# A GNN layer followed by a mixture-of-experts layer on one core: four expert items per turn right behind the last gather, no index translation there, and epochs of 62, 22 and 14 node tiles instead of 54, 30 and 14

## The chip, the cores and the metric

The kernel runs on one core of one Trainium2 chip. The metric is the time of the whole program on the device in microseconds (us). TensorE is called PE here and its weight loads PEld; VectorE is DVE, ScalarE is ACT, GpSimd is POOL, and SyncE is SP, which in this kernel only issues DMAs. SPq, ACTq and POOLq are the instruction streams that issue DMAs.

## What is computed

There are 12,500 nodes with 256 features each and 212,500 weighted edges, sorted by their target node. Everything is float32.

```python
x = x + gnn(layernorm(x), src, dst, edge_weight, W, b)
#   msgs = f[src] * edge_weight; agg = segment_sum(msgs, dst); agg @ W.T + b
x = x + ffn(layernorm(x), gate_w, gate_b, W1, b1, W2, b2)
#   probs = softmax(x @ gate_w + gate_b); the two largest of 8 experts are kept
#   out  += prob[e] * (gelu(x @ W1[e] + b1[e]) @ W2[e] + b2[e])   (256 -> 512 -> 256)
```

## The kernel before, in words

**Tiles and turns.** The edges are cut into 208 groups of 1,024 (`NG`), the nodes into 98 tiles of 128 (`NT`). A planner (`plan`) writes out a list of turns before the kernel is built. Every engine's program is the same list of turns, each engine doing its own part in a fixed order, and semaphores tie them together. A turn below 208 is "busy": POOL gathers the 1,024 source rows of one group with eight indirect DMAs (`gather`, L523), DVE makes the eight 128x80 masks of the group (L1366), PE multiplies them with the rows (`sums`, L885), and the 80 sums are turned and added into a ring of node columns (L875, L1379). `rows` has three buffers, so POOL can be up to three groups ahead of PE.

**Nodes.** When all edges of a tile are in, the tile goes through the linear layer (`linear`, L905), the second layernorm (`node` on DVE, `normalise` on ACT) and the gate (`turn_node` L924, `logits` L933). Tiles are routed in parts (`SIZES`, 2 to 8 tiles): `softmax`, `choose`, `rank` (PE, L941), `place` (DVE) decide for each token which expert's queue it goes to and at which row.

**Queues.** Each tile is then sorted by expert on PE (`sort`, L913), copied by ACT (L1123) and stored to a staging area in memory; from there `copy_some_runs` (L504) copies eight runs, one per expert, into the queues `slots`. SP issues them; from tile 92 on SP and POOL issue four each. `send` is SP's name for it.

**Items.** A block of 128 queued tokens of one expert is an item. An item is open when all its tokens are sure to be sent. It takes four steps: SP loads it and its expert's first matrix (`load_xi`, L688 and L691), PE turns it (`turn_xi`, L949), `up` multiplies it with W1 (L962), `gelu` on ACT (L1166), `down` multiplies with W2 (L978), and `result` on DVE adds the bias and scales (L1590, L1593). In the planner a step is a tuple `(a, b, c, entering)`: item `a` goes down, `b` up, `c` is turned and `entering` is loaded. In a busy turn there is one step, or two in every second turn while more than six items wait; in a turn behind the last gather there are two, and three once all tiles are sent. There are 217 items.

**Epochs and results.** The tiles are cut into three epochs (`EPOCH_SIZES`). Queues are filled up to whole blocks at the end of an epoch, so that the results of one epoch can be read back while later ones are still built. Results of the first two epochs go to memory by item (`store_y`, `yq`). A node's two results are found by `index_results` on DVE (L1604 to L1608, called the translation here) and fetched by POOL with two indirect DMAs per tile (`gather_results`, L564): one tile per busy turn (`got`), four tiles per turn, called a batch, behind the last gather (`pairs`, made of the same `rows` and `got` buffers). DVE adds them to the node's row (L1612, L1614) and SP stores the output (L747, L720). Results of the third epoch are scattered instead, one indirect DMA per item (`scatter_result`, L551), and read at the very end (`finish_late`, L738): SP issues those reads when all scatters and the output stores of the last three batches have landed.

The order inside a turn behind the last gather is written in `tail_turn`, once for each engine. There SP loads all the turn's items first and sends tiles after that. A tile that is routed and sent within the same turn stands in `t.quick`; `t.index` are the tiles translated in the turn.

## Time and profile before

| | before |
|---|---|
| median of 3 runs | 2578.02 us (2567.03, 2578.02, 2579.33) |
| the profiled execution | 2568.56 us, span 2566.9 us |
| mean granted TensorE clock | 0.91 |
| busy: PE, POOL, PEld, DVE, ACT | 81%, 70%, 63%, 62%, 25% of the span |
| last gather of source rows issued | 2290.20 us |
| last scatter of a result issued | 2541.52 us |

The span runs from the first to the last instruction; the execution's own time is 1.7 us longer. The busy share is that of instructions at work: an indirect DMA counts 0.95 us on POOL, but the next one starts 1.25 us after it, so a POOL that does nothing but issue them shows 76%.

### The profile page before, as it was taken

The page shows a single profiled execution, that of the slowest core. Times are in us where ns is not written, and L with a number is a line of the kernel's source. Part 1 is how long each engine was busy: PE and PEld are TensorE (multiplying, and loading weights), DVE is VectorE, ACT ScalarE, POOL GpSimd, SP SyncE. Part 2 cuts the span into 40 slices and gives each one's busy share as a digit, 9 for nine tenths or more (in the row PEclk, how much of TensorE's full clock was granted, in tenths as well). Part 3 has the DMA queues.
Part 4 walks back from the last instruction along what each step waited for, and adds up shares of the span by engine and source line. Part 5 has one row for each costly group of instructions (what it writes and reads, how often), then busy time and mean ns, then how long its engine had stood idle before and what let it go on. Part 6 is the DMA issues. An engine that isn't in the chain of part 4 may idle for free.

```text
span 2566.9 us, 46927 instructions
## 1 busy us (share of the span) xinstructions
PE 2069.9 (81%) x11178; PEld 1625.8 (63%) x11179; DVE 1591.4 (62%) x6566; ACT 653.7 (25%) x1900; POOL 1802.5 (70%) x1909
## 2 busy tenths in 40 slices
PE   4666786688899889888897899896978878886595
PEld 2444564477677677765775678674757666765485
DVE  7888546446565465465666756776776656776344
ACT  3332111122222122221321223221223222232131
POOL 7665777777777777777767767577777777752473
PEclk8776888899999999998999999998989889998797
DMA  8766755867868879778788699597889788795696
GB/s 285 250 206 211 233 176 167 258 217 250 292 215 272 262 222 293 255 233 271 221 263 274 200 302 299 171 307 251 272 275 315 230 272 281 262 284 199 221 370 227
DMA packets 304350, 646.04 MB, mean 252 GB/s; under 512 B 62536, under 2 KB 197226, under 8 KB 291402
## 3 DMA queue, kind: packets, MB, share of 16 engines
q1 hardware_dynamic: 145320, 325.55, 37.4%
q0 software_dynamic: 90384, 248.17, 32.2%
q10 hardware_dynamic: 68370, 69.23, 7.7%
q8 instruction: 100, 1.64, 0.3%
q14 instruction: 176, 1.44, 0.2%
HBM read 543.70 MB, written 208.20 MB: 293 GB/s over the span
## 4 chain that ended last, share of the span: by engine, by line
POOL 26%; PE 19%; DVE 18%; issue 14%; DMA 11%; SPq 11%; ACT 1%; DVEq 1%; ACTq 0%; POOLq 0%
POOL rows L523 22%; SPq L504 8%; PE bank L885 7%; DMA slots<-stage 5%; PE bank L978 5%; PE bank L962 4%; DMA stage<-sorted_x 3%; POOL got L564 2%; DVE spread L1366 2%; DVE bn L1345 2%; SPq L454 1%; PE bank L905 1%; DVE pre_bn L1322 1%; DVE square_n L1413 1%; POOL rows L564 1%
## 5 line engine op out<-in xcount | busy, mean ns | idle before, releaser
L523 POOL DMA_INDIRECT rows<-xhat,src_t x1488 | 1423.0, 956 | 500.8 <-issue 446.2
L885 PE MATMUL bank<-rows,spread 128*80 128x256 f32 x3328 | 870.4, 421 | 163.4 <-DMA rows<-xhat,src_t 70.8
L885 PEld LDWEIGHTS bank<-rows,spread 128*80 128x80 f32 x3328 | 548.7, 168 | 445.7 <-issue 200.7
L978 PE MATMUL bank<-w,hT 128*128 x1736 | 439.1, 398 | 46.3 <-DVE y_sb L1593 29.0
L962 PEld LDWEIGHTS bank<-xiT,w 128*128 128x128 f32 x3472 | 423.9, 193 | 28.6 <-issue 8.2
L962 PE MATMUL bank<-xiT,w 128*128 128x128 f32 x3472 | 427.7, 277 | 9.8 <-ACT xiT L1150 5.6
L1166 ACT ACTIVATE hT<-bank,b1T 128x128 f32<-128x128 f32 x868 | 247.6, 368 | 672.7 <-PE bank L962 455.5
L978 PEld LDWEIGHTS bank<-w,hT 128*128 128x128 f32 x1736 | 326.8, 198 | 101.0 <-issue 61.7
L1379 DVE TENSOR_TENSOR acc<-acc,bank 128x160 f32 x208 | 66.9, 322 | 506.8 <-PE bank L875 455.7
L1366 DVE TENSOR_SCALAR spread<-iota_w,dst_rel,wgt 128x80 f32<-128x80 f32 x1488 | 366.2, 338 | 0.2
L523 POOL DMA_INDIRECT rows<-in_x,src_t x176 | 168.4, 957 | 75.9 <-issue 51.0
L1590 DVE TENSOR_TENSOR y_sb<-bank,b2B 128x256 f32<-128x256 f32 x217 | 91.5, 422 | 181.2 <-PE bank L978 171.6
L1110 ACT ACTIVATE sums_n<-bank 80x256 f32<-80x256 f32 x186 | 69.7, 375 | 385.8 <-PE bank L885 385.6
L913 PE MATMUL bank<-xs,sort_mask 128*128 128x272 f32 x392 | 133.5, 423 | 29.7 <-DVE sort_mask L1532 25.6
L1116 ACT ACTIVATE xs<-x_t,shift,rstd 128x256 f32<-128x256 f32 x98 | 59.3, 605 | 344.2 <-DVE shift L1416 340.0
L564 POOL DMA_INDIRECT got<-yq,gather_i x120 | 115.7, 964 | 36.6 <-issue 36.3
L875 PE MATMUL bank<-ident,sums_n 80*128 80x80 f32 x416 | 68.6, 247 | 82.1 <-ACT sums_n L1108 51.0
L905 PE MATMUL bank<-gnn_wT,acc 128*128 128x256 f32 x392 | 109.5, 404 | 19.9 <-DVE acc L1379 19.9
L1123 ACT ACTIVATE sorted_x<-bank 128x272 f32<-128x272 f32 x196 | 77.4, 395 | 169.9 <-PE bank L913 158.1
L875 PEld LDWEIGHTS bank<-ident,sums_n 80*128 80x128 f32 x416 | 49.3, 144 | 106.8 <-ACT sums_n L1108 53.9
L949 PE MATMUL bank<-ident,xi 128*128 128x128 f32 x434 | 85.3, 279 | 36.5 <-DMA xi<-slots 36.5
L933 PEld LDWEIGHTS bank<-gate_wS,xnT 128*128 128x128 f32 x392 | 59.5, 208 | 83.6 <-ACT xnT L1140 80.8
(191 smaller groups left out, 1893.3 us busy)
## 6 DMA issues: line engine op xcount, KB each, us to landing
w<-in_w SPq DMA_DIRECT2D x217, 512.0 KB
slots<-stage SPq DMA_DIRECT2D x760, 136.0 KB
xi<-slots SPq DMA_DIRECT2D x217, 136.0 KB
stage<-sorted_x ACTq DMA_DIRECT2D x98, 272.0 KB
rows<-xhat,src_t POOLq DMA_INDIRECT x1488
yq<-y_sb ACTq DMA_DIRECT2D x182, 128.0 KB
x_t<-in_x SPq DMA_DIRECT2D x97, 128.0 KB
x_d<-x_t ACTq DMA_DIRECT2D x97, 128.0 KB
```

Of the source, the lines that this page charges most:

```text
L504: eng.dma_start(slots[bass.ds(b, P), :], stages[t % STAGES][bass.ds(a, P), :]).then_inc(done, 16)
L523: pool.indirect_dma_start(rows[q][:, c, :], None, x if g < RAW else xhat, bass.IndirectOffsetOnAxis(ap=src_t[:, g * CG + c:g * CG + c + 1] ...
L564: pool.indirect_dma_start(to[:, c, :], None, yq[0:FIRST_ITEM[EPOCH_OF[PART_OF[t]] + 1] * P], bass.IndirectOffsetOnAxis(ap=gather_i[:, t, c ...
L875: done = nc.tensor.transpose(B_TURN[:, k * W:(k + 1) * W], sums_n[:, k * P:(k + 1) * P], ident[0:W, 0:W])
L885: done = nc.tensor.matmul(B_SUM[0:W, 0:D], spread[g % 2][:, c, :], rows[q][:, c, :], start=c == 0, stop=c == CG - 1)
L905: done = nc.tensor.matmul(B_NODE[:, 0:D], tile(t)[:, k, :], gnn_wT[:, k, :], start=k == 0, stop=k == KD - 1)
L913: nc.tensor.matmul(B_SORT[:, 0:XW], sort_mask[t % 2][:, h * P:(h + 1) * P], xs[:, t % XR, :], start=True, stop=True).then_inc(sort_done, 1)
L962: done = nc.tensor.matmul(bank[:, j * P:(j + 1) * P], w1[:, i % W1B, b, j * P:(j + 1) * P], xiT[i % 2][:, b, :], start=b == 0, stop=b == K ...
L978: done = nc.tensor.matmul(bank[:, 0:D], hT[i % 2][:, j, :], w2[:, bass.ds(e, 1), j, :].rearrange("p o f -> p (o f)"), start=j == 0, stop=j ...
L1166: done = nc.scalar.activation(hT[i % 2][:, j, :], bank[:, j * P:(j + 1) * P], ACT.Gelu, bias=b1T[:, bass.ds(e * KH + j, 1)])
L1366: done = nc.vector.tensor_scalar(spread[g % 2][:, c, :], iota_w[:], dst_rel[:, g * CG + c:g * CG + c + 1], w8[:, c:c + 1] if g < RAW else ...
L1590: nc.vector.tensor_tensor(y_sb[i % YB][:], bank[:, 0:D], b2B[:, bass.ds(e, 1), :].rearrange("p o f -> p (o f)"), op=ALU.add).then_inc(y_bi ...
```

## The change

Three edits and the reordering that they need:

1. `EPOCH_SIZES`: the first epoch has 62 tiles (131 items) in place of 54 (115), the second 22 (51) in place of 30 (67). The third is the same (35 items).
2. In turns behind the last gather, until the last tile is sent, up to four items enter in place of two. The third and fourth step stand behind the sorting of the turn's quick tiles on PE and ACT; on SP their loads stand behind the sending of the quick tiles.
3. The translation is left out of those turns (turns 208 to 210); in the turns behind them two tiles are translated per turn.

```diff
-EPOCH_SIZES = ((6, 8, 8, 8, 8, 8, 8), (8, 8, 6, 4, 4), (4, 4, 2, 2, 2))
+EPOCH_SIZES = ((6, 8, 8, 8, 8, 8, 8, 8), (8, 8, 6), (4, 4, 2, 2, 2))
...
-        n_steps = (1 + (waiting > 6 and tau % 2 == 0)) if busy else 2 if NK - 1 not in sent_at else 3
+        n_steps = (1 + (waiting > 6 and tau % 2 == 0)) if busy else min(4, max(2, waiting)) if NK - 1 not in sent_at and with_sums else 3
...
-        while index_next < LATE and len(t.index) < (1 if busy else BATCH):
+        while index_next < LATE and len(t.index) < (1 if busy or not with_sums else 2 if NK - 1 in sent_at else 0):
...
             def tail_turn(plan, t, last_turns, fast, first_batched):   # SP
-                for step in t.steps:
+                for step in t.steps[:2]:
                     if step[3] >= 0:
                         load_xi(step[3])
...
-                for u in ([t.stage] if t.stage >= 0 else []) + t.quick:
-                    send(u)
+                if t.stage >= 0:
+                    send(t.stage)
+                for step in [] if t.quick else t.steps[2:]:
+                    if step[3] >= 0:
+                        load_xi(step[3])
...
+                for u in t.quick:
+                    send(u)
+                for step in t.steps[2:] if t.quick else []:
+                    if step[3] >= 0:
+                        load_xi(step[3])
...
-                for a, b, c, _ in t.steps[1:]:                         # PE
+                for a, b, c, _ in t.steps[1:2]:
                     if b >= 0:
                         up(b, fast)
                     step_down(a, c, fast)
                 for u in t.quick:
                     sort(u, 0)
                     sort(u, 1)
+                for a, b, c, _ in t.steps[2:]:
+                    if b >= 0:
+                        up(b, fast)
+                    step_down(a, c, fast)
```

ACT is split in the same way as PE. The new list of turns differs from the old one as follows. Up to turn 139 nothing moves but translations. The first tile's results are fetched in turn 177 in place of 160, so that 31 tiles are fetched in busy turns in place of 48, and 53 behind them in place of 36 (14 batches in place of 10). Busy turns with two steps are turns 132 to 138, 152 to 172, 184 to 188 and 196 to 206 (each second one) in place of 134 to 154, 166 to 172, 178 to 186 and 194 to 204. 170 items are through at the end of the busy turns in place of 176. The four turns 208 to 211 have 4, 4, 4 and 3 steps in place of 2, 2, 2 and 3, so that both plans stand at the same item (184) at the end of turn 210. The list has 226 turns in place of 225.

The order of the instructions shows it at three places.

PE at the end of turn 208 and the start of turn 209, before. L913 is the sort of tile 93, L941 and L942 rank the part of tiles 92 and 93, L875 turns the last group's sums, L905 is the linear layer of tile 96:

```order
L978 MATMUL bank<-w,hT 128x256
L913 MATMUL bank<-xs,sort_mask 128x272 x2
L941 MATMUL bank<-both,below 128x16
L942 MATMUL bank<-both,ones 128x16
L875 MATMUL bank<-ident,sums_n 128x80 x2
L962 MATMUL bank<-xiT,w 128x128 x8
L905 MATMUL bank<-gnn_wT,acc 128x256 x2
```

The same place in the changed kernel (its lines stand eight further down: L921 is the sort, L957 turns an item, L949 and L950 rank):

```order
L921 MATMUL bank<-xs,sort_mask 128x272 x2
L970 MATMUL bank<-xiT,w 128x128 x8
L957 MATMUL bank<-ident,xi 128x128 x2
L978 TENSOR_LOAD item_be
...
L970 MATMUL bank<-xiT,w 128x128 x8
L957 MATMUL bank<-ident,xi 128x128 x2
...
L949 MATMUL bank<-both,below 128x16
L950 MATMUL bank<-both,ones 128x16
L883 MATMUL bank<-ident,sums_n 128x80 x2
L970 MATMUL bank<-xiT,w 128x128 x8
L913 MATMUL bank<-gnn_wT,acc 128x256 x2
```

Two whole steps, with an item to be turned in each, now stand between the sort and the next turn's rank and linear layer.

SP in turn 208, before, where the copies of the quick tile (L504) are the turn's last transfers but for one output, and the next turn's items follow:

```order
L504 DMA slots<-stage 16x2176
L747 DMA out_nodes<-res 128x256
L454 TENSOR_LOAD item_be
L688 ISA
L688 DMA xi<-slots 128x272
L691 ISA
L691 DMA w<-in_w 128x1024
```

The same place in the changed kernel:

```order
L504 ISA
L504 DMA slots<-stage 16x2176
L454 TENSOR_LOAD item_be
L688 ISA
L688 DMA xi<-slots 128x272
L691 ISA
L691 DMA w<-in_w 128x1024
```

The store of the output has moved ahead of the copies, four loads of items follow instead of two, and the first two of them belong to turn 208 itself: the fourth step of that turn turns the first of them on PE.

POOL at the end of the program, before (L551 scatters results of the third epoch, L564 fetches results):

```order
L551 DMA results<-y_sb,result_i 27136x256 x3
L564 DMA rows<-yq,gather_i 128x256 x8
L551 DMA results<-y_sb,result_i 27136x256 x3
L564 DMA rows<-yq,gather_i 128x256 x4
L551 DMA results<-y_sb,result_i 27136x256 x11
```

The same place in the changed kernel:

```order
L551 DMA results<-y_sb,result_i 27136x256 x3
L564 DMA rows<-yq,gather_i 128x256 x8
L551 DMA results<-y_sb,result_i 27136x256 x3
L564 DMA rows<-yq,gather_i 128x256 x4
L564 DMA got<-yq,gather_i 128x256 x4
L551 DMA results<-y_sb,result_i 27136x256 x2
L564 DMA got<-yq,gather_i 128x256 x2
```

The last eleven scatters had no fetches between them; now fetches go on until behind the last scatter.

## Rows read from the trace of the kernel before

**Rows 1.** The page's busy time of each engine.

```profile
PE 2069.9 (81%) x11178; PEld 1625.8 (63%) x11179; DVE 1591.4 (62%) x6566; ACT 653.7 (25%) x1900; POOL 1802.5 (70%) x1909
```

**Rows 2.** Busy time of each engine by stage; last PEclk, DMA share, GB/s.

```profile
1455.94:1674.54 218.60, 201.06 (x1185) 166.66 (x1184) 146.86 (x583) 62.09 (x196) 143.98 (x152) 0.98 0.78 253
...
1900.88:2293.69 392.81, 334.88 (x1821) 268.46 (x1822) 259.29 (x1060) 101.35 (x304) 298.65 (x310) 0.92 0.83 271
2293.69:2401.69 108.00, 72.11 (x370) 58.76 (x369) 65.38 (x289) 29.08 (x80) 19.53 (x33) 0.83 0.56 179
2401.69:2516.36 114.67, 93.73 (x612) 85.86 (x613) 46.52 (x146) 33.01 (x116) 85.29 (x88) 0.90 0.99 348
```

**Rows 3.** POOL in order of time: turns 160, 177, last busy fetch, tail.

```profile
1684.55 0.95 POOL L523 DMA_INDIRECT rows<-xhat,src_t  x1 [0.30 <-issue]
...
1900.88 0.95 POOL L523 DMA_INDIRECT rows<-xhat,src_t  x1 [0.30 <-issue]
...
2292.73 0.95 POOL L564 DMA_INDIRECT got<-yq,gather_i  x1 [0.30 <-issue]
...
2401.69 1.01 POOL L564 DMA_INDIRECT rows<-yq,gather_i  x1 [0.30 <-issue]
...
2541.52 0.96 POOL L551 DMA_INDIRECT results<-y_sb,result_i  x1 [0.77 <-DVE y_sb L1593]
```

**Rows 4.** POOL's waits for PE in 1455.94-1590.67, to 1674.54, to 2293.69: total, times, longest.

```profile
POOL rows L523 <- PE bank L885: 16.7, 8, 3.9
...
POOL rows L523 <- PE bank L885: 14.8, 4, 8.4
...
POOL rows L523 <- PE bank L885: 0.3, 1, 0.3
```

**Rows 5.** PE in order of time: sums of three successive groups (turns 153 to 155).

```profile
1605.02 3.62 PE L885 MATMUL bank<-rows,spread 128*80 128x256 f32 x16
...
1616.76 3.65 PE L885 MATMUL bank<-rows,spread 128*80 128x256 f32 x16
...
1625.03 1.24 PE L885 MATMUL bank<-rows,spread 128*80 128x256 f32 x5
```

**Rows 6.** PE in order of time behind the last gather.

```profile
2321.88 2.05 PE L905 MATMUL bank<-gnn_wT,acc 128*128 128x256 f32 x4 [5.41 <-DVE acc L1379]
...
2342.15 0.64 PE L924 MATMUL bank<-ident,xs 128*128 128x128 f32 x2
...
2359.80 0.69 PE L949 MATMUL bank<-ident,xi 128*128 128x128 f32 x2 [9.15 <-DMA xi<-slots]
...
2364.23 0.45 PE L941 MATMUL bank<-both,below 128*128 128x16 f32 x2
...
2385.58 0.87 PE L913 MATMUL bank<-xs,sort_mask 128*128 128x272 f32 x2
```

**Rows 7.** DVE in order of time: first translation of turn 208, its last, `place` of turn 211.

```profile
2314.02 0.28 DVE L1604 SCALAR_TENSOR_TENSOR item_hit<-item_all,block_of,item_row 128x67 f32<-128x67 f32 x1
...
2320.05 0.17 DVE L1608 CAST gather_i<-item_of 128x2 int32<-128x2 f32 x1
...
2375.37 0.15 DVE L1477 COPY count_et<-bank 128x16 f32<-128x16 f32 x1
```

**Rows 8.** SP's DMA issues in order of time: start, length, transfer.

```profile
2307.81 12.15 SPq L504 DMA_DIRECT2D slots<-stage  x8
...
2341.81 12.11 SPq L504 DMA_DIRECT2D slots<-stage  x8
...
2355.26 0.33 SPq L688 DMA_DIRECT2D xi<-slots  x1
...
2544.66 6.09 SPq L738 DMA_DIRECT2D rows<-results  x12
```

**Rows 9.** DMA issues by line: count, KB each, median us from issue to landing.

```profile
out_nodes<-res SPq DMA_DIRECT2D x60, 128.0 KB, 4.0
...
rows<-yq,gather_i POOLq DMA_INDIRECT x48, 5.8
```

More of the change, by code:

```diff
@@ L1194, in tail_turn @@
                     copy_sums(t.sums)
-                for _, b, c, _ in t.steps[1:]:
+                for _, b, c, _ in t.steps[1:2]:
                     if b >= 0:
@@ L1206, in tail_turn @@
                     store_sorted(u)
+                for _, b, c, _ in t.steps[2:]:
+                    if b >= 0:
+                        gelu(b, fast)
+                    if c >= 0:
+                        copy_xiT(c)
             def turns(plan, fast):
```

## The prediction

> **What bounds the kernel now.** The page's busy shares come first, and they mislead: PE leads with 81%, POOL has 70% [rows 1]. The list of POOL's instructions in time says otherwise. In busy turns each indirect DMA starts 0.3 us behind the end of the one before, whose reason is "issue", that is, nothing but its own sequencer. The stage table gives the pace: 310 DMAs in 392.81 us, 1.267 us each [rows 2]. A busy turn with a fetch has ten of them, so the 17 turns 160 to 176 take 216.33 us, 12.73 us each [rows 3]; with eight it cannot be below 10.0. The list of POOL's waits then shows where PE ends a wait of POOL: 16.7 us in turns 140 to 151, 14.8 us in turns 152 to 158, and 0.3 us in the 619 us behind that, where the longer turns leave PE slack [rows 4]. So POOL's issue rate sets the busy stage, PE only in patches before the fetches begin.
>
> Behind the last gather the picture has three stages. For 108 us POOL is busy 19.5 us and PE 72.1 [rows 2]: the last tiles are made, routed, sorted and sent, a chain of short steps with many engines. From 2401.69 to 2516.36 POOL issues without a pause again: 88 DMAs in 114.67 us, 1.303 us each. Then come the last scatters, the last at 2541.52 [rows 3], and SP's reads of the scattered results at 2544.66 [rows 8], 22.2 us before the span's end.
>
> **The busy stage: about 30 us shorter.** 17 tiles are no longer fetched there: 34 DMAs x 1.267 = 43.1 us of POOL's issue. This is the gain if POOL stays the bound. PE corrects it. A turn with two steps takes PE 11.74 us from one group's sums to the next, one with one step 8.27 [rows 5]: the double costs 3.5 us. I work out the four patches.
> - Turns 140 to 151 lose their doubles (the planner runs out of open items, since the longer epoch opens its last block later). POOL's 8 waits there, 16.7 us less the usual 0.3 us for each, 14.3 us, go: -14.3.
> - Turns 152 to 158: the 14.8 us, 13.6 net, fall at the routing of a part of eight tiles. The same routing stands there after the change, so nothing goes; two more doubles (156, 158) with sorts beside them: +7.
> - Turns 160 to 163 are now 10 us turns with two doubles and sorts: +7. Doubles without a sort beside them fit, since 11.74 + 8.27 is two turns of POOL.
> - The routing of the next eight tiles (turns 170 to 173) now also falls in 10 us turns. It cost nothing at 12.7 us; at 10 us it cost 13.6 in the patch above: +13.6.
>
> -43.1 - 14.3 + 7 + 7 + 13.6 = -30. The bounds: if PE never makes POOL wait, -43.1 - 27.9 = -71. If each of the nine doubles of turns 156 to 172 costs 3.5, -43.1 - 14.3 + 31.5 + 13.6 = -12. I take -30, as doubles with a sort did cost that much and those without did not.
>
> **The routing chain behind the last gather: about 20 us longer.** Here both plans reach the same item by turn 210, so six items (21 us of PE at 3.5) come in, and twelve translations go out. What the translations cost is seen in DVE: four of them take from 2314.02 to 2320.22, 1.55 us each, and the linear layer of tile 96 waits 5.41 us for the addition behind them [rows 6, 7]. That wait goes. What comes in its place:
> - Turn 208. Two steps are put between the sort of tile 93 and the rank and linear layer of turn 209, 7 us, and the second of them turns an item whose load SP issues only behind the copies of tile 93. These end at 2319.96; an item is turned 4.5 us after its load is issued (2355.26 to 2359.80, [rows 6, 8]). So PE stands at that item until about 2325.5, and behind it on its queue are rank, the last sums' turn and the linear layer. That goes to about 2331 from 2321.88: +9.
> - Turn 209. The same, and worse: the copies of tiles 94 and 95 keep SP for 12.11 us [rows 8], which is 9 us later now, to about 2363; its two loads follow, the item is there at 2369, one more down step, and turn 210's first gate transpose, the one that everything in the routing of tiles 96 and 97 hangs on, is at about 2372 instead of 2342.15 [rows 6]: +30.
> - Turn 210. Before, PE waited 9.15 us here for the item behind these same copies; that wait is now served already. Two more steps cost 7. Rank at about 2391 instead of 2364.23: +27.
> - Turn 211. Before, DVE took 11.1 us from that rank to `place`, of which four translations are 6.2 [rows 6, 7]. They are gone; the listing stays. From `place` to the sort of tile 96 it is 10.2 us as before. Sort at about 2406 instead of 2385.58: +20.
>
> The last stall is the same as before in kind: the third load of turn 211 stands behind the last copies. Bounds: below, the items hide in PE's 35.9 idle us and only the translation's wait goes, -6; above, the whole slip of turn 209 stays, +30. I take +20.
>
> Were the load quicker, less would be lost. The trace has 4.5 us from its issue to the start of the transpose. The Trainium skill, "DMA: Bandwidth & Descriptors", Anatomy of one DMA, gives 2.0 us plus the bytes at 436 GB/s, 2.3 us for 136 KB, fitted on DMAs that GpSimd issues; by that page of the Trainium skill each of the two stalls would be 2.2 us shorter and the chain +16. The row decides here.
>
> **The stage that POOL bounds at the end: about 41 us longer.** POOL starts batch 1 when tile 97 is copied (2401.69 before). From there to the end of the last scatter (2542.48) it issued 64 fetches and 35 scatters in 140.8 us. Now it has 98 fetches (53 tiles, less the four of batch 0) and 35 scatters: 133 x 1.303 = 173.3 us, +32.5. PE needs 3.5 us for an item and has three per turn of about 14 us, so it follows. The 25 us in which POOL used to wait for the last items are filled with fetches. Then the end: the late reads started 2.2 us behind the last scatter. Now the last thing is a fetch, whose landing, addition and output store come first: 5.8 us from issue to landing, of which 0.95 is issue, 0.9 us on DVE, 0.6 us of SP's issue, 4.0 us to land [rows 9]. That makes 10.4, +8.2. Together +40.7. Bounds: +35 if the pace is 1.25 and the store lands at once, +46 if batches wait for buffers.
>
> **Sum.** -30 + 20 + 41 = +31 us on the profiled execution's own 2568.56 (span 2566.9): 2600. The runs shown lie at two places, 2567.0 and 2578 to 2579, the profiled one at the lower; on the median, 2578.0, the sum is 2609. I forecast the middle, 2604. About 0.5% (13 us) is what a measurement of this kernel can tell from no change.
>
> **The rivals.**
> - *The moved items hide.* PE is idle 35.9 us in the 108 us stage [rows 2], the six items need 21. If they fall into its waits, the chain is -6 in place of +20: -30 - 6 + 41 = +5, 2574 to 2583, no change. For it: the room. Against it: PE runs in order, and the loads stand behind SP's copies. The Trainium skill, "Perfetto Trace Analysis", Optimization Strategy, speaks for this rival: where the most-contended engine changes over time, interleaving those regimes may improve performance.
> - *POOL never waits for PE in the busy stage*, so that this is at its bound of -71. That is one mechanism, three row buffers bridging the routing of turns 155 and 172, and it ends on the other side: -71 + 20 + 35 = -16, 2562 on the median. It decides from a busy saving of about 68 us on. Against it: the waits of 8.4 us in just such a turn [rows 4].
> - *More stalls than I count.* A PE that waits comes back slow: the granted clock is 0.83 in the 108 us stage, against 0.98 in the dense one [rows 2], and the DMA share of 0.99 behind it leaves no room for transfers that bunch. Chain +30, busy -20: +51, 2629.
> - *The fetches cost nothing at the end*, because PE is the bound there. Then +8 in place of +41: -2, no change. The row against it is POOL's unbroken issue from 2401.69 to 2516.36.
>
> **How the numbers follow.** My forecast 0.58, more stalls 0.15, items hide 0.11, fetches free 0.04, POOL never waits 0.08, something else 0.04, half of it slower and half faster. Slower 0.75, same 0.15, faster 0.10. The range of 8 in 10 leaves out the upper end of the stalls and most of the faster case: 2574 to 2630; the forecast's own range is 2590 to 2622.
>
> **What the profile of the changed kernel would show.** Right: the last gather of source rows issued near 2260; turns 140 to 151 at 10.0 us with no wait for PE, turns 173 and 174 with waits of 5 to 8 us; PE waiting for `xi` from `slots` in turns 208 and 209; 135 to 145 us from the last busy fetch to POOL's batch 1, against 109; then POOL issuing unbroken for about 170 us, and the late reads some 10 us behind the last fetch. Wrong: a POOL with pauses in that last stage, or a PE without waits for `xi` in turns 208 and 209.

## The result, and the profile after

| | before | after |
|---|---|---|
| median of the runs | 2578.09 us (6 runs, 2567.03 to 2582.58) | 2595.35 us (6 runs, 2588.18 to 2602.12) |
| profiled execution, own time | 2568.56 us | 2600.76 us |
| span of it | 2566.9 us | 2599.2 us |

The changed kernel is slower: ratio 1.0082, 95% interval 1.0064 to 1.0099, so 16 to 26 us. The forecast was 2604 us with 2574 to 2630, slower with a chance of 0.75.

The page's busy line of the changed kernel hardly differs from [rows 1]; it can't tell where 32 us went:

```profile
PE 2076.3 (80%) x11174; PEld 1626.9 (63%) x11175; DVE 1584.5 (61%) x6506; ACT 652.6 (25%) x1897; POOL 1802.2 (69%) x1909
```

Busy time by stage of the changed kernel, columns as in [rows 2]. The stages are turns 140 to 159, turns 160 to 176, the other turns with gathers, the chain behind them, the stage of the batches, and what follows the start of the late reads:

```profile
1453.95:1673.76 219.81, 181.31 (x958) 140.52 (x957) 141.49 (x570) 49.59 (x148) 152.84 (x160) 0.93 0.72 227
1673.76:1875.03 201.27, 183.01 (x1074) 149.94 (x1074) 131.26 (x516) 56.36 (x179) 130.14 (x136) 0.99 0.79 255
1875.03:2268.41 393.38, 323.38 (x1752) 255.86 (x1750) 280.57 (x1120) 99.69 (x295) 298.99 (x310) 0.92 0.86 279
2268.41:2395.05 126.64, 93.73 (x504) 77.27 (x504) 52.52 (x223) 36.94 (x107) 19.55 (x32) 0.84 0.59 191
2395.05:2576.31 181.26, 124.77 (x796) 113.42 (x796) 95.07 (x328) 42.63 (x150) 129.76 (x133) 0.86 0.88 298
2576.31:2599.20 22.89, 0.00 (x0) 0.00 (x0) 8.86 (x10) 0.00 (x0) 0.00 (x0) 0.50 0.73 236
```

Against [rows 2, 3, 8]: everything up to the end of turn 207 is 25.3 us shorter (2268.41 for 2293.69), the chain 18.6 us longer (126.64 for 108.00), the stage of the batches 38.3 us longer (181.26 for 142.97), and the rest 0.7. The sum is +32.3, the difference of the two spans. In the fifth row GpSimd issues 133 DMAs in 181 us, as counted in the prediction.

GpSimd's waits for TensorE in turns 140 to 151, 152 to 159, 160 to 176 and behind them (total, times, longest), which answer to [rows 4]:

```profile
POOL rows L523 <- PE bank L893: 7.7, 2, 7.4
...
POOL rows L523 <- PE bank L893: 11.8, 3, 6.5
...
POOL rows L523 <- PE bank L893: 33.6, 13, 7.2
...
POOL rows L523 <- PE bank L893: 0.6, 2, 0.3
```

The third row is new: 33.6 us in thirteen waits, where before had one, of 0.3 us. The first row is not empty, as the prediction had it: a wait of 7.4 us stays in turn 141. TensorE behind the last gather, which answers to [rows 6]: the item of turn 208 whose load is late, the linear layer of tile 96, the late item of turn 209, the gate transpose of tile 96, the rank, and the sort of tile 96.

```profile
2297.98 0.69 PE L957 MATMUL bank<-ident,xi 128*128 128x128 f32 x2 [4.58 <-DMA xi<-slots]
...
2305.76 1.10 PE L913 MATMUL bank<-gnn_wT,acc 128*128 128x256 f32 x4 [0.58 <-DVE acc L1396]
...
2342.85 0.69 PE L957 MATMUL bank<-ident,xi 128*128 128x128 f32 x2 [9.14 <-DMA xi<-slots]
...
2347.28 0.40 PE L932 MATMUL bank<-ident,xs 128*128 128x128 f32 x2
...
2365.30 0.29 PE L949 MATMUL bank<-both,below 128*128 128x16 f32 x2
...
2377.55 0.86 PE L921 MATMUL bank<-xs,sort_mask 128*128 128x272 f32 x2 [4.18 <-DVE sort_mask L1549]
```

SyncE's queue shows why the second item is late: its load (2337.59) stands behind the copies of tiles 94 and 95, which answer to the 12.11 us of [rows 8].

```profile
2325.64 11.24 SPq L504 DMA_DIRECT2D slots<-stage  x8
2337.59 0.34 SPq L688 DMA_DIRECT2D xi<-slots  x1
```

The item is turned 5.26 us after that issue (2342.85).

### The profile page after: what moved, and what is told of

Same layout as the page of the kernel before. It is cut to its first block, busy times and chain, and to the rows that moved or that the text cites. A ratio compares the mean times of both kernels' runs of the same rounds, so it can differ in the third digit from the quotient of the medians.

```text
span 2599.2 us, 46816 instructions
## 1 busy us (share of the span) xinstructions
PE 2076.3 (80%) x11174; PEld 1626.9 (63%) x11175; DVE 1584.5 (61%) x6506; ACT 652.6 (25%) x1897; POOL 1802.2 (69%) x1909
## 4 chain that ended last, share of the span: by engine, by line
POOL 23%; PE 19%; DVE 17%; issue 14%; DMA 13%; SPq 11%; ACT 1%; DVEq 1%; ACTq 1%; POOLq 0%
POOL rows L523 19%; SPq L504 9%; PE bank L893 8%; DMA slots<-stage 7%; PE bank L986 4%; PE bank L970 4%; DMA stage<-sorted_x 2%; POOL got L564 2%; DVE spread L1383 2%; DMA rows<-xhat,src_t 1%; DVE bn L1362 1%; POOL rows L564 1%; SPq L454 1%; PE bank L913 1%; POOL results L551 1%
## 5 line engine op out<-in xcount | busy, mean ns | idle before, releaser
L921 PE MATMUL bank<-xs,sort_mask 128*128 128x272 f32 x392 | 133.5, 423 | 27.4 <-DVE sort_mask L1549 23.3
L564 POOL DMA_INDIRECT got<-yq,gather_i x104 | 100.9, 970 | 31.7 <-issue 31.7
L913 PE MATMUL bank<-gnn_wT,acc 128*128 128x256 f32 x392 | 110.1, 405 | 12.9 <-DVE acc L1396 12.9
L957 PE MATMUL bank<-ident,xi 128*128 128x128 f32 x434 | 85.3, 279 | 34.7 <-DMA xi<-slots 34.6
L941 PEld LDWEIGHTS bank<-gate_wS,xnT 128*128 128x128 f32 x392 | 58.9, 206 | 85.5 <-ACT xnT L1152 83.0
```

The lines of the kernel that those rows point to most:

```text
L564: pool.indirect_dma_start(to[:, c, :], None, yq[0:FIRST_ITEM[EPOCH_OF[PART_OF[t]] + 1] * P], bass.IndirectOffsetOnAxis(ap=gather_i[:, t, c ...
L913: done = nc.tensor.matmul(B_NODE[:, 0:D], tile(t)[:, k, :], gnn_wT[:, k, :], start=k == 0, stop=k == KD - 1)
L921: nc.tensor.matmul(B_SORT[:, 0:XW], sort_mask[t % 2][:, h * P:(h + 1) * P], xs[:, t % XR, :], start=True, stop=True).then_inc(sort_done, 1)
```

## The experiments

Every kernel was timed against the kernel before on the same chip; those named e and those named f in the table ran on two different chips, so they are compared by these ratios. To read them I cut each profile at three events: the end of the last gather of source rows on GpSimd; GpSimd's copy behind its last wait of 4 to 7 us for earlier copies to land, 2.8 us ahead of its next fetch; and the start of SyncE's late reads. For the changed kernel the first two are

```profile
2264.73 0.94 POOL L523 DMA_INDIRECT rows<-xhat,src_t  x1 [0.30 <-issue]
...
2392.28 0.49 POOL L504 DMA_DIRECT2D slots<-stage  x1 [6.10 <-DMA slots<-stage]
```

| kernel | ratio to before (95%) | last gather ends | chain | batches | PE matmuls in them |
|---|---|---|---|---|---|
| before | 1 | 2291.2 | 107.8 | 145.8 | 770 |
| changed | 1.0082 (1.0064-1.0099) | 2265.7 | 126.6 | 184.0 | 796 |
| e1, changed with old epochs | 1.0017 (1.0001-1.0033) | 2293.8 | 122.2 | 135.7 | 640 |
| e2, new epochs alone | 1.0032 (1.0016-1.0048) | 2261.9 | 104.8 | 187.2 | 926 |
| e7, translation rule alone | 0.9956 (0.9941-0.9972) | 2294.8 | 89.3 | 150.3 | 770 |
| e3, changed, loads ahead of copies | 1.0005 (0.9989-1.0020) | 2258.1 | 107.5 | 179.7 | 789 |
| f1, changed, half the batch fetches | 1.0001 (0.9987-1.0016) | 2264.0 | 122.0 | 157.6 | 798 |
| f3, e3 with old epochs | 0.9925 (0.9905-0.9945) | 2296.2 | 102.8 | 134.4 | 637 |
| f4, e7 and a batch a turn earlier | 0.9996 (0.9980-1.0011) | 2295.2 | 107.0 | 149.4 | 770 |
| f2, e7 with four epochs | 1.0124 (1.0098-1.0150) | 2352.4 | 91.7 | 142.8 | 770 |

Behind the late reads all have 22 to 23 us. The column of the last gather has its own scatter: kernels whose turns 0 to 207 do the same work lie at 2291.2 to 2296.2 and at 2258.1 to 2265.7. So a difference of 5 us there says nothing.

**e1: the epochs of before put back.**

```diff
-EPOCH_SIZES = ((6, 8, 8, 8, 8, 8, 8, 8), (8, 8, 6), (4, 4, 2, 2, 2))
+EPOCH_SIZES = ((6, 8, 8, 8, 8, 8, 8), (8, 8, 6, 4, 4), (4, 4, 2, 2, 2))
```

> The changed kernel with the epochs of before (54, 30 and 14 tiles): only the third and fourth steps and the translation rule are new. Theory (the chain behind the last gather grew by the extra steps ahead of the sorts, and the epochs alone moved fetches out of the turns with gathers and into the end): the stage with gathers is as before (-2 to +1 us), the stretch from the last gather to the first fetch batch is 17 to 19 us longer, the end is 4 us shorter since more items are through when the batches begin; together 13 to 15 us over the kernel before, a ratio near 1.005. Rival 1 (the extra steps are the whole of the loss and the epochs cost nothing in sum): about +28 to +31 us, ratio 1.011 to 1.012. Rival 2 (extra steps lie in idle time of TensorE): -6 to 0 us.

Measured 1.0017, +4 us (0 to 8). The chain grew by 14.5 us, near what was expected; the stage of the batches fell by 10 us, not 4. The first rival (the steps are the whole loss) is out: with the new epochs in place of the old the same kernel is 17 us slower. Why the items removed were worth so much is taken up under f3.

**e2: the new epochs alone.** The same line changed in the kernel before.

> The kernel before with the epochs of 62, 22 and 14 tiles and nothing else. Theory: the stage with gathers is 25 us shorter, as in the changed kernel (33 fetch instructions fewer ahead of the last gather, less the stalls of new two-step turns), the chain from the last gather to the first batch is as before (within 3 us), and the end takes 42 to 47 us more, since GpSimd issues 33 fetch instructions more there at 1.3 us each; together +18 to +22 us, ratio 1.007 to 1.0085. Rival 1 (GpSimd does not bound the end, and fetches moved there are hidden): -25 us, ratio 0.990. Rival 2 (the epochs are neutral, what GpSimd gains it gives back one for one): 0 us.

Measured 1.0032, +8 us (4 to 12), under the expected 18 to 22. Both parts are there: the last gather 29 us earlier, the batches 41 us longer, the chain 3 us shorter. I had taken 25 and 42 to 47 and hung the expectation on the before's profiled execution, whose last gather is the earliest of the five with old epochs. Averaged over five and four profiles (2294.2 and 2262.4) the epochs bring 31.8 us there.

**e7: the translation rule alone.**

```diff
-        while index_next < LATE and len(t.index) < (1 if busy else BATCH):
+        while index_next < LATE and len(t.index) < (1 if busy or not with_sums else 2 if NK - 1 in sent_at else 0):
```

> The kernel before with the translation rule of the changed kernel alone: none in the three turns behind the last gather, two per turn behind. Theory: VectorE has its translations off the chain there (TensorE's wait of 5.41 us for the sums of tile 96 and VectorE's 6.2 us ahead of the places go), so the stretch from the last gather to the first batch is 6 to 12 us shorter, and nothing else moves: -6 to -12 us, ratio 0.995 to 0.998. Rival: the translations were in idle time of VectorE and the chain is set by the copies to the store and the index loads on the queues: 0 us, ratio 1.000. Second rival: the translations that are late keep GpSimd's batches waiting at the end: +5 us.

Measured 0.9956, -11 us (7 to 15): this part of the change is a gain by itself. TensorE's linear layer of tile 96, the rank and the sort of tile 96:

```profile
2317.48 1.03 PE L905 MATMUL bank<-gnn_wT,acc 128*128 128x256 f32 x4
...
2358.62 0.45 PE L941 MATMUL bank<-both,below 128*128 128x16 f32 x2
...
2371.99 0.62 PE L913 MATMUL bank<-xs,sort_mask 128*128 128x272 f32 x2
```

Counted from the last gather's end these are 22.6, 63.8 and 77.2 us; in before [rows 6] 30.7, 73.1 and 94.4. The wait for the addition is gone, which with what stood around it is 8.1 us, and from rank to sort it is 13.4 us in place of 21.3. That is more than the 6.2 us that the translations take on VectorE. Most of the rest is on TensorE: the eight matmuls of an item's down step, which stand right ahead of that sort, take 3.78 us in before, behind 7.05 us of idle time, and 1.99 us in e7, behind 1.16 us:

```profile
2382.01 3.78 PE L978 MATMUL bank<-w,hT 128*128 x8 [7.05 <-DVE y_sb L1593]
```

```profile
2370.16 1.99 PE L978 MATMUL bank<-w,hT 128*128 x8 [1.16 <-ACT hT L1166]
```

The granted clock is 0.50 in the first of these stretches, the lower of its two levels, and 1.00 in the second. So with the idle time of the wait goes 1.8 us of slower matmuls. Of the chain's 18.5 us, 4.5 are lost again in the batches, where GpSimd waits 24.0 us for item results in place of 18.8.

**e3: the changed kernel, with SyncE issuing all loads of items ahead of its copies.**

```diff
-                for step in t.steps[:2]:
+                for step in t.steps:
                     if step[3] >= 0:
                         load_xi(step[3])
...
-                for step in [] if t.quick else t.steps[2:]:
-                    if step[3] >= 0:
-                        load_xi(step[3])
```

(and the same three lines behind the sends of `t.quick`).

> The changed kernel with SyncE issuing all index loads of a turn ahead of its copies to the store, as the kernel before did, in place of behind them. Theory: the waits of TensorE for the loaded item indices in the two turns behind the last gather (4.58 and 9.14 us) vanish, the copies start 1 to 3 us later; net 7 to 10 us shorter than the changed kernel, ratio to the kernel before near 1.005. Rival 1 (the waits only move: the linear step or the sort that comes next waits for the later copies, or for VectorE): no difference to the changed kernel, ratio 1.008. Rival 2 (the later copies delay the sorted index and then the first batch): +3 us.

Measured 1.0005 against 1.0082: 20 us shorter than the changed kernel, twice what was expected. All of it is in the chain (107.5 for 126.6) and the batches (179.7 for 184.0). The two waits for `xi` are gone, and the same events of TensorE are:

```profile
2291.12 1.10 PE L907 MATMUL bank<-gnn_wT,acc 128*128 128x256 f32 x4 [0.86 <-DVE acc L1390]
...
2338.55 0.29 PE L943 MATMUL bank<-both,below 128*128 128x16 f32 x2
...
2350.82 1.28 PE L915 MATMUL bank<-xs,sort_mask 128*128 128x272 f32 x2 [4.20 <-DVE sort_mask L1543]
```

From the last gather: 33.0, 80.4 and 92.7 us; in the changed kernel 40.1, 99.6 and 111.9. The waits of the rows (4.58 + 9.14) are less than the 19.2 us they cost, because each queue waits for the other: SyncE's copies of tiles 94 and 95 wait for tiles that TensorE sorts, and TensorE stands at an item whose load is behind SyncE's copies. In e3 the third load of turn 209 goes out 35.3 us behind the last gather, in the changed kernel 71.9 (the 2337.59 above); the copies of 94 and 95 start at 52.9 us in e3 and at 60.0 in the changed kernel (2325.64):

```profile
2293.39 0.33 SPq L688 DMA_DIRECT2D xi<-slots  x1
...
2311.04 10.61 SPq L504 DMA_DIRECT2D slots<-stage  x8
```

In e3 the chain is as long as in before, with five to six items more in it (527 matmuls for 385, 26 to an item). TensorE's busy time in it, 91.68 us of 107.45, stands against 72.11 of 108.00 in [rows 2]:

```profile
2258.13:2365.58 107.45, 91.68 (x527) 77.21 (x526) 53.07 (x226) 37.95 (x112) 19.73 (x31) 0.89 0.69 227
```

That does not show the items hidden in TensorE's idle time, since the chain of before also holds the translations. Against e7, which has none either, e3's chain is 18.2 us longer (107.5 for 89.3), close to the 21 us that the prediction gives to six items.

The Trainium skill, "Perfetto Trace Analysis", Optimization Strategy, says that interleaving regimes with different busiest engines may improve performance. By that rule items moved into the chain should pay. Whether they do with the loads in time is read from f3 against e7, below, and by those two the trace agrees, if by little.

**f1: half of the fetches behind the last gather left out.** One of the two results of each of those nodes is left out of the output.

```diff
-                for c in range(2):
+                for c in range(2 if done in got_in else 1):
...
-                dve.wait_ge(batch_got[t.batch % BATCHES], 32 * batch_loads(plan, t.batch))
+                dve.wait_ge(batch_got[t.batch % BATCHES], 16 * batch_loads(plan, t.batch))
```

> The kernel of the run that fetches only one of a node's two results behind the last gather (that result of those nodes is left out of the output), again, on another chip, since the first chip ran every kernel, the one before too, some 36% slower. The expectation stands: with GpSimd's issue as the bound of the last stage, its 53 DMAs fewer take 69 us off until TensorE's own items stop it, 2550 to 2565 us; if TensorE bounds the stage, within 5 us of the changed kernel (ratio 1.008).

Measured 1.0001 against 1.0082, 21 us less, between the theory and its rival. The batches take 157.6 us for 184.0. GpSimd's rows in turn show why they stop there: it waits for item results in every turn.

```profile
2476.90 0.98 POOL L551 DMA_INDIRECT results<-y_sb,result_i  x1 [1.74 <-DVE y_sb L1610]
2478.45 0.97 POOL L551 DMA_INDIRECT results<-y_sb,result_i  x1 [0.56 <-DVE y_sb L1610]
2480.41 0.96 POOL L551 DMA_INDIRECT results<-y_sb,result_i  x1 [0.99 <-DVE y_sb L1610]
```

GpSimd's waits for item results in the stage of the batches (total, times, longest), of before, changed, f1, f3:

```profile
POOL results L551 <- DVE y_sb L1593: 18.8, 13, 3.4
```

```profile
POOL results L551 <- DVE y_sb L1610: 7.4, 4, 2.8
```

```profile
POOL results L551 <- DVE y_sb L1610: 47.3, 30, 6.9
```

```profile
POOL results L551 <- DVE y_sb L1604: 12.8, 9, 5.2
```

So GpSimd does bound the end of the changed kernel, but by 26 us only (184.0 - 157.6); below that stand the items. In fetches that is about 20, at the 1.303 us of [rows 2], of the 34 that the epochs moved there.

**f3: old epochs, translation rule, up to four steps, loads ahead of the copies.** e3 with the first diff of e1. First run as e10, below.

> The old epochs with the translation rule, up to four steps, and all loads ahead of the copies, again, on another chip. Theory (the extra steps cost TensorE's own time on the chain, given back in part at the end): ratio 0.998 to 1.001, against 0.9956 of the translation rule alone. Rival (with the loads in time the steps are hidden, and fewer items are left at the end): 0.992 to 0.9945.

Measured 0.9925, -19 us (14 to 24): the best kernel here, in the range of the rival and not of my expectation. Beside e7 the steps cost the chain 13.5 us, as expected (12 to 20), but the batches gave back 15.9, not 4 to 9. There are 133 matmuls fewer there, 26 to an item, so five items, and GpSimd's waits for results fall from 24.0 us (e7) to 12.8. GpSimd also has less to issue: six of its 35 scatters stand in the chain already, the first of them

```profile
2357.20 1.04 POOL L551 DMA_INDIRECT results<-y_sb,result_i  x1 [0.30 <-issue]
```

where in e7 the first follows 7.9 us behind the copy that ends the chain. At 1.3 us each they are some 8 us of GpSimd's time in the stage. How the 15.9 us divide between the items and the scatters no run separates. e1 has the same six scatters ahead of its batches, which fits their being 10 us shorter and not 4. With the new epochs no scatter moves and GpSimd hardly waits for results (7.4 us), so the same items are worth less there: 187.2 us in e2, 184.0 in the changed kernel and 179.7 in e3.

The profile alone gives -1 us against e7; the two timed ratios differ by 8 us, on two chips, with intervals that touch, so it is likely, not certain, that the extra steps are a gain.

**f4: e7 with the first batch a turn earlier.**

```diff
-        most = 1 if busy else BATCH if tau >= NG + 2 or not with_sums else 0
+        most = 1 if busy else BATCH if tau >= NG + 1 or not with_sums else 0
```

> The kernel before with the translation rule of the changed kernel, and the first batch of fetches one turn earlier, in the turn right behind the last one of gathers but one (four tiles in turn 209, two in turn 210, in place of four and two in turns 210 and 211). Theory: GpSimd is idle there between the last gathers and the scatters of the last tiles, so four DMAs of the last stage (a batch of two tiles) move into idle time, 5 us less at the end, VectorE's additions of turn 210 stand ahead of the listing, +2 to +3 us of the chain: -2 to -4 us against the translation rule alone, ratio 0.994 to 0.995. Rival (each batch holds VectorE's and SyncE's queue ahead of the routing): +3 to +8 us, ratio 0.997 to 0.999.

Measured 0.9996, 10 us over e7; the rival was right in kind, and the loss is larger than its 3 to 8 us. The chain is 17.7 us longer (6 of them stand there already at turn 208, ahead of anything the edit moves) and the batches no shorter. In the chain that ended last the batch stands in the middle of the routing: eight fetches from 2356.25, 6.65 us for the last to land, then VectorE's additions.

```profile
2365.10 6.65 DMA rows<-yq,gather_i
2371.84 0.43 DVE rows L1612
```

**f2: four epochs of 46, 16, 22 and 14 tiles on e7**, so that fetches begin at turn 143 and 62 tiles are through by the last gather.

```diff
-EPOCH_SIZES = ((6, 8, 8, 8, 8, 8, 8), (8, 8, 6, 4, 4), (4, 4, 2, 2, 2))
+EPOCH_SIZES = ((6, 8, 8, 8, 8, 8), (8, 8), (8, 6, 4, 4), (4, 4, 2, 2, 2))
```

> The four epochs of 46, 16, 22 and 14 tiles again, on another chip. On the slow one it was 2.2% over the kernel before, where GpSimd did not bound the stage with gathers (1303 us of its time idle, 705 of it for TensorE, in a kernel of the same call), so that seven items more had their full price. Theory: where GpSimd is the bound, the fetches that start at turn 143 lie in its waits for TensorE, and the end is 28 DMAs shorter: -2 to -20 us against the kernel with the translation rule alone, ratio to the kernel before 0.988 to 0.995. Rival (TensorE's items are the price here as well): 7 items x 3.5 us = 25 us, and two turns more until the first batch: ratio 1.003 to 1.015.

Measured 1.0124; the rival was right. No turn from 143 on has a wait for TensorE of more than 0.3 us, as hoped, but the first epoch's items now come as two-step turns into the 10 us turns ahead of it: turns 120 to 139 turn 28 items in place of 17 (e7), GpSimd waits 1.7 to 3.9 us for TensorE in every second turn from 127 to 139, and turn 140 begins at 1496.5 us in place of 1460.8. That is 35.7 of the 57.6 us by which the last gather is later. And the stage of the batches gained 7.5 us against e7. Of the 28 fetches fewer, 20 are missing in that stage (26 us at 1.303) and eight in the chain; GpSimd now waits longer for item results in their place (24.0 us in e7):

```profile
POOL results L551 <- DVE y_sb L1593: 41.8, 18, 5.4
```

**Four runs on another chip.** e4 is the kernel of f1, e8 that of f2, e10 that of f3, and e6 has one step in turns 156 to 176. That chip ran every kernel some 36% slower, the one before too (3506 us). In a profile of it (e6) GpSimd's gather DMA still takes 953 ns, but GpSimd is idle 1303 us ahead of them, 705 of it for TensorE, at a mean granted clock of 0.82 for 0.91. GpSimd is not the bound there, so these say little on this change.

> The changed kernel, but the batches behind the last gather fetch only one of a node's two results, so that result of those nodes is left out of the output (the other is added as before; VectorE adds what stands in the buffer). GpSimd issues 53 DMAs fewer in the last stage, 96 from where 149 stood behind the first of them. Theory (GpSimd's issue bounds that stage): the stretch falls by 53 x 1.3 = 69 us until TensorE's own work stops it, at about 140 us from the start of the batches to the late reads in place of 181; so -30 to -45 us against the changed kernel, 2550 to 2565 us. Rival (TensorE or the queues bound it, GpSimd only looks full): within 5 us of the changed kernel. Second rival (the gap between DMAs of one engine grows when there are fewer, since the DMA engines are the bound): -10 to -20 us.

Ratio 0.9849 (0.9794 to 0.9905).

> The kernel before with the translation rule of the changed one and four epochs of 46, 16, 22 and 14 tiles: fetches begin at turn 143 in place of 160 and 62 tiles are through by the last gather in place of 48; seven items more in all (224 for 217), batches begin two turns later. Theory (the epochs of the changed kernel went the wrong way: GpSimd waits for TensorE some 30 us in turns 140 to 158, fetches put there lie in those waits, and each fetch less at the end saves 1.3 us): the stage with gathers +35 us for 28 DMAs, less 15 to 28 us of waits that they fill, +8 to +20; the end -28 x 1.3 = -36 us, +5 to +10 for the later first batch; net against the kernel with the translation rule alone (2562.3 us) -2 to -20 us, so 2542 to 2560, ratio 0.988 to 0.995. Rival 1 (the seven items more cost TensorE 3.5 us each, and it comes to be the bound where it is at 83% now): +5 to +20 against it, 2567 to 2582. Rival 2 (fetches cost the same in either place and nothing is hidden): +5, since one epoch more costs its table and its tail.

Ratio 1.0224 (1.0184 to 1.0263).

> The kernel before with the translation rule and up to four steps in a turn behind the last gather, SyncE's loads ahead of its copies as before, the third and fourth step behind the sorts as in the changed kernel: it differs from the kernel with the translation rule alone by the extra steps. Theory (the extra steps lengthen the chain of routing by TensorE's own time, since they stand ahead of the rank and the linear layer on its queue, and give back a part at the end, where fewer items are left): chain +12 to +20 us, end -4 to -9 us; about +5 to +12 against the kernel with the translation rule alone (2562.3 us), so 2567 to 2574, ratio 0.998 to 1.001. Rival 1 (with the loads in time the steps hide in TensorE's idle time): -4 to -9 us against it, 2553 to 2558. Rival 2 (the order of SyncE's loads was not the cause; the stalls come with any extra step): chain +30, about 2585.

Ratio 0.9996 (0.9954 to 1.0037).

```diff
-        n_steps = (1 + (waiting > 6 and tau % 2 == 0)) if busy else ...
+        n_steps = (1 + (waiting > 6 and tau % 2 == 0 and not 155 < tau < 177)) if busy else ...
```

> The changed kernel without two-step turns in turns 156 to 176: items are completed later, so the first epoch is finished later and fetches begin later in the turns with gathers. Theory (the two-step turns make GpSimd wait for TensorE there, with or without a sort beside them): GpSimd's waits for TensorE in turns 156 to 172 are gone but for those at the routing of a part, so those turns take 10.0 to 10.1 us in place of 10.1 to 13.4, 15 to 20 us less; the fetches missing there are issued at the end, +15 to +25 us; net -3 to +8 us against the changed kernel. Rival (the waits are caused by the routing alone and the doubles fit into the slack of one-step turns): turns 156 to 172 stay as they are, and the whole is +15 to +25 us over the changed kernel.

Ratio 1.0024 (0.9988 to 1.0060). e6 was not run elsewhere, nor was the changed kernel run on that chip: what the two-step turns cost is read from the waits in the rows below and in f2 only.

## Why the prediction was right

**Busy stage, forecast -30: -25.3 in the two profiles, -31.8 by the averages.** The pieces inside were sized wrongly and made up for each other; that their sum came out is in part luck. Turns 140 to 151 fell by 6.4 us in the two profiles and 8.7 in the averages, not by 14.3, since a wait of 7.4 us stays in turn 141. Turns 152 to 159 fell by 2.4 and 4.6 us where +7 was forecast. Turns 160 to 176 fell by 15.1 and 14.7 us, not 22.5. Another 4.7 us of the averages lie ahead of turn 140, where the plans are the same but for translations and the forecast had nothing; that is within the scatter of this column. The failed step is "I take -30, as doubles with a sort did cost that much and those without did not". Those without a sort cost too. Of GpSimd's waits behind the double turns in turns 161 to 173, the first three (3.70, 3.67 and 3.16 us) have a sort beside the second step. The other four have none, TensorE's last sort of that part being at 1733.18:

```profile
1756.38 0.94 POOL L523 DMA_INDIRECT rows<-xhat,src_t  x1 [2.93 <-PE bank L893]
...
1778.33 0.94 POOL L523 DMA_INDIRECT rows<-xhat,src_t  x1 [1.76 <-PE bank L893]
...
1800.02 0.95 POOL L523 DMA_INDIRECT rows<-xhat,src_t  x1 [1.76 <-PE bank L893]
...
1822.00 0.94 POOL L523 DMA_INDIRECT rows<-xhat,src_t  x1 [1.76 <-PE bank L893]
```

Less the usual 0.3 us for each these four are 7.0 us, most of the 7.4 that were missing. The three with a sort are 9.6 us where two were counted with 7. The argument that 11.74 + 8.27 is two turns of GpSimd left no slack at all: here two such turns of TensorE take 21.7 us (1774.44 to 1796.13), and GpSimd's take 20.0. The routing in a 10 us turn was right: waits of 7.20 and 5.92 us.

**Chain, forecast +20: +18.6.** The events came as written: linear layer of tile 96 +9.2 against the end of turn 207 (forecast +9), gate transpose +30.4 (+30), rank +26.4 (+27), sort +17.3 (+20). Right in sum, and the mechanism, loads behind copies on SyncE's in-order queue, is shown by e3. The prediction's own sign for it, 135 to 145 us from the last busy fetch to batch 1, did not fit this sum (108 + 20) and did not come: it was 127. And the parts of the chain were too small in both directions. The translations, taken off, are worth 18.5 us of chain (e7), 1.8 of them TensorE's clock, where I had 5.4 and 6.2; the steps' own time costs 13.5 to 18 (f3, e3, each against e7); the order of the loads 19.2 (changed against e3). The forecast followed one thread of events through the new order and so landed on their sum without separating them (-18.5 + 18.2 + 19.2).

Here I had weighed a load's time: the Trainium skill, "DMA: Bandwidth & Descriptors", Anatomy of one DMA, would give 2.3 us; by it the chain would be 4 us shorter than forecast. That fit of the Trainium skill is for DMAs issued by GpSimd, and this load is issued by SyncE. The changed kernel shows 5.26 us from issue to use, so the trace does not agree, and the forecast by the older row (4.5) held.

**End, forecast +41: +38.3** (e2: +41.4, cut at the copy). The count of 133 DMAs is as forecast. With the waits for results they took 175.3 us from first to last, forecast 173.3. The mis-sized term is the very end: the last fetch is issued at 2570.32 and the late reads start 6.0 us later (2576.31), not 10.4. The fetch is added 3.3 us behind its issue, not 5.8 and more, and the late reads start 1.8 us behind the end of that work on VectorE (2574.50), so they can't have waited 4.0 us for the store to land. SyncE issues that store at 2574.53 and then waits 1.2 us for it; the shortest landing of such a store in this trace is 1.8 us.

```profile
2570.32 0.97 POOL L564 DMA_INDIRECT got<-yq,gather_i  x1 [0.30 <-issue]
```

```profile
2573.61 0.42 DVE L1629 TENSOR_TENSOR res<-res,got 128x256 f32<-128x256 f32 x1 [2.38 <-DMA got<-yq,gather_i]
2574.07 0.43 DVE L1631 TENSOR_TENSOR res<-res,got 128x256 f32<-128x256 f32 x1
...
2576.31 1.93 SPq L738 DMA_DIRECT2D rows<-results  x4
```

**Sum, +31: +32.3 between the two profiles, +17 between the medians, 16 to 26 by the ratio.** Before's profiled execution was one of the quick ones (its last gather 3 us ahead of the mean of the five, the changed kernel's 3 us behind the mean of its four), so the two profiles overstate the effect. On the median of before the forecast sum gives 2609, 14 us too much. That 2604 lies nearer comes of "I forecast the middle", which no row decided. 2595 is inside the forecast's own range.

**The rivals.** "The moved items hide" was wrong for this kernel. e3 has the time that it names (no change), but by another way: its chain is 18.2 us longer than e7's, so the items are not hidden, and the translations' 18.5 us pay for them. "The fetches cost nothing at the end" is out by f1 and e2. "GpSimd never waits for TensorE" is out by 33.6 us of waits. "More stalls" did not come.

What the change was, then: a rule for translations that gains 11 us; epochs that lose 8 by themselves (they take 32 from one stage in which GpSimd is the bound and put 41 into another) and more beside the extra steps, 17 in the changed kernel (against e1) and 21 in e3 (against f3), since items removed from an end that GpSimd bounds shorten it less; and up to four steps, which gain 1 to 8 us with the loads ahead of the copies (f3 against e7) and lose some 16 with them behind (e1 against e7). f3 keeps the first and the third part, with the loads ahead, and is 1.6% faster than the changed kernel by the two ratios, some 40 us. Whether GpSimd's work could leave the end in another way was not tried.

## What to carry to other kernels

Work moved into the idle time of one engine brings its loads along, and these stand in an order on a queue: put the loads of what is wanted first ahead of copies that wait for the engine that will want them. Before moving work between two stages, see whether the same engine bounds both (then nothing is won), and how far below it the next engine lies, since this is all that taking work away can win. A change of several parts is worth running part by part: here one gain and two losses hid in one ratio.

## What the runs showed of the hardware that was not expected

GpSimd took 1.33 us for each indirect DMA of the last stage (175.3 us for 132, 7.4 us of waits in it) with the DMA engines at a share of 0.88, and 1.30 in before at 0.99 [rows 2]. Without the waits it is 1.28, and 1.27 in the turns with gathers at 0.83 [rows 2]: the load of the DMA engines makes 3% at most here. Its shown busy time of some 0.97 us for each makes an engine that bounds the stage look 72% busy (129.76 of 181.26). And one of the chips used ran the same kernels 36% slower, with the gather DMA as long as elsewhere (953 ns) and the idle time between longer; its cause is open. A step of eight matmuls took 3.78 us behind 7.05 us of idle time and 1.99 behind 1.16 (e7, above): here a wait of TensorE cost a second time in the matmuls behind it.
